# Sigmoid stage of an FFN with fake-quantized activations: six of the twelve gate pieces rounded and multiplied on GpSimd as int32 in place

## The reference

```python
def act_qdq(x):                      # ACT_BITS = 16
    qmax = 2.0 ** (ACT_BITS - 1) - 1.0
    scale = jnp.maximum(jnp.max(jnp.abs(x)) / qmax, 1e-12)
    return jnp.clip(jnp.round(x / scale), -qmax - 1.0, qmax) * scale

def fixed_qdq_u16(x):
    scale = 1.0 / 65536.0
    return jnp.clip(jnp.round(x / scale), 0.0, 65535.0) * scale
...
x = act_qdq(x)
up = act_qdq(x @ lpbq_dequant(w_up).T)
gate = act_qdq(x @ lpbq_dequant(w_gate).T)
sig = fixed_qdq_u16(jax.nn.sigmoid(gate))
gate = act_qdq(gate * sig)
o = act_qdq(gate * up)
return o @ lpbq_dequant(w_down).T
```

## Time and profile before

| | |
|---|---|
| median of 3 runs | 400.63 us |
| profiled execution, span from the first to the last instruction | 398.5 us |
| PE busy | 346.2 us (87%) |
| DVE busy | 330.8 us (83%) |
| ACT busy | 263.0 us (66%) |
| POOL busy | 223.4 us (56%) |
| sigmoid stage, from the gate's scale to `MX2` | 312.0 to 351.9 us |
| `Q` and the reductions | 354.7 to 369.7 us |
| output parts | 372.0 to the end |

### The profile page before, as it was taken

One profiled execution on the slowest core, in us unless ns is written; L12 is line 12 of the kernel. 1 busy time (PEld: TensorE's weight loads), 2 busy tenths in 40 slices (PEclk: granted clock), 3 DMA queues, 4 the chain that ended last, 5 costly groups with the idle time before them and its releaser, 6 DMA issues.

```text
span 398.5 us, 6226 instructions
## 1 busy us (share of the span) xinstructions
PE 346.2 (87%) x1754; PEld 285.0 (72%) x1754; DVE 330.8 (83%) x700; ACT 263.0 (66%) x339; POOL 223.4 (56%) x400
## 2 busy tenths in 40 slices
PE   8979967999999999999999989999999971005997
PEld 7657744768898989989898977777677650003897
DVE  4588558975999999999999989765689899979894
ACT  3655687866576565666656544555467899999650
POOL 2656885897466473847465023222195568992462
PEclk9998999999999999999999999999999996555999
DMA  6998993955353443535332005100000000000022
GB/s 173 341 398 301 326 314 118 315 161 212 112 202 111 151 168 117 201 106 187 132 127 84 3 2 160 51 2 0 1 2 0 1 0 1 0 0 2 0 108 105
DMA packets 19850, 47.77 MB, mean 120 GB/s; under 512 B 2787, under 2 KB 8934, under 8 KB 17254
## 3 DMA queue, kind: packets, MB, share of 16 engines
q1 hardware_dynamic: 18342, 47.16, 33.8%
q10 hardware_dynamic: 1472, 0.20, 0.3%
HBM read 33.10 MB, written 12.58 MB: 115 GB/s over the span
## 4 chain that ended last, share of the span: by engine, by line
PE 59%; DVE 15%; POOL 8%; issue 6%; DMA 6%; ACT 5%; ACTq 0%; DVEq 0%; SPq 0%; POOLq 0%
PE ps L378 57%; DVE S L755 3%; DMA wscr<-wst 2%; POOL XCh L1542 2%; POOL wst L1545 2%; DMA wdr<-n_L_cond_skill_down_dram 2%; DVE O_i L752 1%; PE ps L375 1%; DMA bsr<-in_L_cond_Bs_dram 1%; DVE G L746 1%; ACT U L1307 1%; POOL C_i L1542 1%; ACT ps L1307 1%; DVE Hl L746 1%; DVE HbS L746 1%
## 5 line engine op out<-in xcount | busy, mean ns | idle before, releaser
L1626 POOL CAST xg<-XT 128x64 fp32r x264 | 81.3, 356 | 52.6 <-DVE Hl L746 25.5
L378 PE MATMUL ps<-xg,Wr 128*128 128x384 f32 (+1 forms) x480 | 98.6, 354 | 0.3 <-issue 0.3
L378 PEld LDWEIGHTS ps<-xg,Wr 128*128 128x128 f32 x480 | 85.8, 188 | 7.5 <-issue 0.6
L1307 ACT ACTIVATE Hh<-HbS 128x512 fp32r<-128x512 f32 (+2 forms) x72 | 56.5, 785 | 46.2 <-DVE HbS L746 45.9
L746 DVE TENSOR_TENSOR HbS<-Gb,ps 128x512 f32<-128x512 f32 (+2 forms) x72 | 63.2, 878 | 21.7 <-PE ps L378 18.6
L1307 ACT ACTIVATE Gb<-ps 128x512 f32<-128x512 f32 (+2 forms) x72 | 54.1, 751 | 30.5 <-PE ps L378 28.7
L746 DVE TENSOR_TENSOR Hl<-HbS,Hh 128x768 fp32r<-128x768 f32 (+2 forms) x57 | 55.2, 969 | 2.3 <-ACT Hh L1307 1.8
L752 DVE SCALAR_TENSOR_TENSOR C<-ps,Wt,C 128x32 f32 x264 | 52.4, 279 | 2.9 <-PE ps L378 2.6
L378 PE MATMUL ps<-XT,SHh 128*128 128x512 f32 x128 | 45.7, 398 | 0.8 <-DVE XT L746 0.4
L1545 POOL TENSOR_TENSOR Hl<-HbS,Hh 128x512 fp32r<-128x512 f32 x15 | 19.7, 1316 | 47.0 <-ACT Hh L1307 46.9
L1307 ACT ACTIVATE ps<-G,S 128x1024 int32<-128x1024 f32 (+1 forms) x29 | 35.6, 1250 | 6.7 <-DVE O_i L752 5.7
(11 more groups left out here) (222 smaller groups left out, 675.7 us busy)
## 6 DMA issues: line engine op xcount, KB each, us to landing
Wr<-wscr SPq DMA_DIRECT2D x20, 1024.0 KB, 4.8
wscr<-wst SPq DMA_DIRECT2D x16, 512.0 KB, 5.9
stg<-n_L_cond_skill_gate_dram SPq DMA_DIRECT2D x8, 256.0 KB, 7.6
stg<-in_L_cond_skill_up_dram SPq DMA_DIRECT2D x8, 256.0 KB, 7.9
wdr<-n_L_cond_skill_down_dram SPq DMA_DIRECT2D x8, 256.0 KB, 5.8
xscr<-X SPq DMA_DIRECT2D x8, 256.0 KB, 6.1
X<-xscr SPq DMA_DIRECT2D x8, 256.0 KB, 4.3
out_dram<-X SPq DMA_DIRECT2D x7, 256.0 KB, 2.0
```

What stands on the lines that cost most here:

```text
L378: return e.matmul(o_, l, r, start=start, stop=stop, skip_group_check=True)
L1307: return e.activation(o_, i_, func, **kw)
L1626: last = e.tensor_copy(xg[:, i % XR, :, T * s:T * s + T].rearrange("p a t -> p a t"), XT[:, :, :, bass.ds(regs[s - a_], 1)].rearrange("p a ...
```

## The change

`POOLED` goes from three pieces (3, 6, 9) to six (2, 4, 5, 7, 9, 10). A pooled piece is now an int32 throughout, in the bytes where its float32 stood: POOL rounds `G` to int32 in place, rounds the sigmoid to int32 in place in `tS` (with a limit of 65535 where a zero was added), and multiplies int32 by int32 in place. The conversions back to float32 are gone, six instructions in all, and so are the copies in `C_i`. ACT rounds six pieces where it rounded nine, and DVE multiplies six where it multiplied nine. Everything that reads a pooled piece afterwards (`m`, `Q`, and the first ACT step of the output) reads it as int32. Piece 11 is no longer split into halves. Since a column part j of G holds pieces of both types, ACT makes it in two or three instructions where it made it in one. The four order strings are written anew, except `PE_ORDER`.

```diff
-        POOLED = (3, 6, 9)
+        POOLED = (2, 4, 5, 7, 9, 10)
+        Gi = Gf.bitcast(I32)
+        tI = tS[:, :, :].bitcast(I32)
...
-        DVE_ORDER = ("gtop gsc r0 r1 r2 r3 y0 m0 r5 r4 y1 r6 m1 y2 r8 r7 r9 y4 r10 r11 um y5 utop m2 usc m4 y7 m3 m5 y8 m7 "
+        DVE_ORDER = ("gtop gsc r0 r1 r2 y0 m0 r3 y1 r4 m1 y3 r5 m3 r6 r7 r8 r9 r10 r11 um m4 utop m5 usc y6 y8 m7 m2 m6 m8 "
...
-        OF = {0: 2, 1: 3, 2: 2, 4: 3, 5: 2, 7: 1, 8: 3, 10: 2, 11: 0}
+        OF = {0: 2, 1: 3, 3: 2, 6: 2, 8: 3, 11: 1}
+        def runs(j):
+            kinds = [4 * q + j // 2 in POOLED for q in range(3)]
+            cuts = [q for q in range(3) if q == 0 or kinds[q] != kinds[q - 1]] + [3]
+            return [(a_, b_, kinds[a_]) for a_, b_ in zip(cuts, cuts[1:])]
...
-                    before = {0: (a_g, 11), 1: (a_g, 13), 7: (a_u, 12), 11: (d_sc, USC)}
-                    after = {2: 0, 4: 1, 5: 2, 8: 4, 10: 5}
+                    before = {0: (a_g, 11), 1: (a_g, 13), 11: (a_u, 12)}
+                    after = {3: 0, 6: 3, 8: 1}
...
-                    do(tS[:, p % 4, c], (C_i[:, pc(POOLED.index(p))] if p in POOLED else sloti(OF[p]))[:, c],
-                       ACT.Sigmoid, scale=col(SG_)).then_inc(a_sig, 1)
+                    do(tS[:, p % 4, :], Gi[:, pc(p)] if p in POOLED else sloti(OF[p]), ACT.Sigmoid, scale=col(SG_)).then_inc(a_sig, 1)
...
-                do(part(j, 0, 4), G[:, :, cols(j)], ACT.Identity, scale=col(I2)).then_inc(a_sgn, 1)
+                for a_, b_, whole in runs(j):
+                    g = G[:, a_:b_, cols(j)]
+                    last = do(part(j, 0, 4)[:, a_:b_, :], g.bitcast(I32) if whole else g, ACT.Identity, scale=col(I2))
+                last.then_inc(a_sgn, 1)
...
                 if kind == "q":
-                    w.wait_ge(d_xcl, (2, 4, 5)[k])
-                    ts(C_i[:, pc(k)], Gf[:, pc(p)], col(IG), 0.0).then_inc(k_gq, 1)
-                    w.wait_ge(k_gq, pooled_nth(step))
-                    ts(Gf[:, pc(p)], C_i[:, pc(k)], 1.0, 0.0).then_inc(k_gf, 1)
+                    ts(Gi[:, pc(p)], Gf[:, pc(p)], col(IG), 0.0).then_inc(k_gq, 1)
                 elif kind == "t":
-                    ts(t_i[:, p % 4, c], tS[:, p % 4, c], 65536.0, 0.0).then_inc(k_t, 1)
                     if p in POOLED:
-                        w.wait_ge(k_t, nth(POOL_ORDER, step))
-                        ts(tS[:, p % 4, :], t_i[:, p % 4, :], 1.0, 0.0).then_inc(k_tf, 1)
+                        ts(tI[:, p % 4, :], tS[:, p % 4, :], 65536.0, 65535.0, MUL, ALU.min).then_inc(k_t, 1)
+                    else:
+                        ...
+                        ts(t_i[:, p % 4, :], tS[:, p % 4, :], 65536.0, 0.0).then_inc(k_t, 1)
                 elif kind == "y":
-                    e.tensor_tensor(Gf[:, pc(p)], Gf[:, pc(p)], tS[:, p % 4, :], MUL).then_inc(k_y, 1)
+                    e.tensor_tensor(Gi[:, pc(p)], Gi[:, pc(p)], tI[:, p % 4, :], MUL).then_inc(k_y, 1)
```

More of the change, by code:

```diff
@@ L232, in program @@
             sem(n) for n in ("p_g", "a_g", "p_u", "a_u", "d_mxg", "d_mxu"))
-        a_gq, k_gq, k_gf, a_sig, k_t, k_tf, d_y, k_y, d_my, a_ua, k_uq, a_yq, d_o = (
-            sem(n) for n in ("a_gq", "k_gq", "k_gf", "a_sig", "k_t", "k_tf", "d_y", "k_y", "d_my", "a_ua", "k_uq", "a_yq", "d_o"))
+        a_gq, k_gq, a_sig, k_t, d_y, k_y, d_my, a_ua, k_uq, a_yq, d_o = (
+            sem(n) for n in ("a_gq", "k_gq", "a_sig", "k_t", "d_y", "k_y", "d_my", "a_ua", "k_uq", "a_yq", "d_o"))
         a_sgn, d_oi, k_of, p_out, d_out = (
@@ L333, in program @@
         PIECE = [4 * q + jp for q, jp in ORDER]
-        POOLED = (3, 6, 9)
+        POOLED = (2, 4, 5, 7, 9, 10)
         Uf = U[:, :, :].rearrange("p k n -> p (k n)")
         Gf = G[:, :, :].rearrange("p k n -> p (k n)")
+        Gi = Gf.bitcast(I32)
+        tI = tS[:, :, :].bitcast(I32)
         U_if = U_i[:, :, :].rearrange("p q n -> p (q n)")
         PE_ORDER = "u0 u1 gt gsp u2 u3 u4 u5 u6 u7 u8 u9 u10 u11 ut usp".split()
-        ACT_ORDER = ("e0 e1 q0 e2 s0 e3 e4 q1 e5 s1 q2 e6 s2 e7 s3 e8 q4 e9 s4 e10 q5 e11 s5 q7 s6 q8 s7 q10 s8 A4 s9 A7 "
-                     "s10 q11 A2 s11a A10 s11b A5 A1 A9 A8 A3 A6 A0 Q0 Q1 Q2 Q3 Q4 Q5 Q6 Q7 Q8 Q9 Q10 A11 Q11").split()
-        DVE_ORDER = ("gtop gsc r0 r1 r2 r3 y0 m0 r5 r4 y1 r6 m1 y2 r8 r7 r9 y4 r10 r11 um y5 utop m2 usc m4 y7 m3 m5 y8 m7 "
-                     "m6 m8 y10 m10 y11b y11a m9 m11a m11b").split()
-        POOL_ORDER = "q6 t0 q3 t1 t2 q9 t3 t4 y3 t5 t6 t7 y6 t8 t9 t10 y9 t11a t11b v0 v1 v2 v3 v4 v5 v6 v7 v8 v9 v10 v11".split()
-        OF = {0: 2, 1: 3, 2: 2, 4: 3, 5: 2, 7: 1, 8: 3, 10: 2, 11: 0}
+        ACT_ORDER = ("e0 e1 q0 e2 s0 s2 q1 e3 s1 s4 q3 e4 s3 e5 e6 s5 e7 e8 q6 e9 e10 s7 e11 q8 s6 s8 q11 s9 s10 A9 s11 A4 A1 "
+                     "A2 A6 A10 A0 A5 A3 A8 A7 Q0 Q1 Q2 Q3 Q4 Q5 Q6 Q7 Q8 Q9 Q10 A11 Q11").split()
+        DVE_ORDER = ("gtop gsc r0 r1 r2 y0 m0 r3 y1 r4 m1 y3 r5 m3 r6 r7 r8 r9 r10 r11 um m4 utop m5 usc y6 y8 m7 m2 m6 m8 "
+                     "y11 m11 m9 m10").split()
+        POOL_ORDER = ("q7 q2 t0 t2 q4 q9 t1 q5 q10 t4 t3 t5 y2 y5 y4 t7 t6 t8 y7 t9 t11 y9 t10 y10 "
+                      "v0 v1 v2 v3 v4 v5 v6 v7 v8 v9 v10 v11").split()
+        OF = {0: 2, 1: 3, 3: 2, 6: 2, 8: 3, 11: 1}
         def nth(order, step):
@@ L1219, in _ @@
             for step_ in DVE_ORDER:
-                kind, h = step_[0], step_[-1] if step_[-1] in "ab" else ""
+                kind = step_[0]
                 if step_ == "gtop":
@@ L1250, in _ @@
                     else:
[L1251 to L1254, removed]
+                        w.wait_ge(d_y, nth(DVE_ORDER, f"y{p}"))
+                    red(S[:, G2M + p:G2M + p + 1], (Gi if p in POOLED else Gf)[:, pc(p)], ALU.max, True).then_inc(d_my, 1)
+            w.wait_ge(d_my, 12)
+            red(col(MX2), S[:, G2M:G2M + 12], ALU.max).then_inc(d_col, 1)
             top(4, bank[7])
@@ L1499, in _ @@
             for step in ACT_ORDER:
-                kind, h = step[0], step[-1] if step[-1] in "ab" else ""
-                p = int(step[1:].rstrip("ab"))
+                kind, p = step[0], int(step[1:])
                 if kind == "e":
@@ L1512, in _ @@
                 elif kind == "s":
-                    c = HALF[h]
                     if p in POOLED:
@@ L1666, in _ @@
                 elif kind == "t":
-                    w.wait_ge(a_sig, nth(ACT_ORDER, "s" + step[1:]))
-                    if p >= 4:
-                        w.wait_ge(*((k_y, pooled_nth(f"y{p - 4}")) if p - 4 in POOLED else (d_y, nth(DVE_ORDER, f"y{p - 4}"))))
-                    ts(t_i[:, p % 4, c], tS[:, p % 4, c], 65536.0, 0.0).then_inc(k_t, 1)
+                    w.wait_ge(a_sig, nth(ACT_ORDER, step.replace("t", "s")))
                     if p in POOLED:
-                        w.wait_ge(k_t, nth(POOL_ORDER, step))
-                        ts(tS[:, p % 4, :], t_i[:, p % 4, :], 1.0, 0.0).then_inc(k_tf, 1)
+                        ts(tI[:, p % 4, :], tS[:, p % 4, :], 65536.0, 65535.0, MUL, ALU.min).then_inc(k_t, 1)
+                    else:
+                        for o_ in (p - 4, p - 8):
+                            if o_ >= 0 and o_ not in POOLED:
+                                w.wait_ge(d_y, nth(DVE_ORDER, f"y{o_}"))
+                        ts(t_i[:, p % 4, :], tS[:, p % 4, :], 65536.0, 0.0).then_inc(k_t, 1)
```

26 lines of the change are left out of this document (11 added, 15 removed).

## The result

The changed kernel took 411.37 us (median of 4 runs, 410.69 to 412.50) against 400.79 before in the same comparison: a ratio of 1.0273, 95% interval 1.0241 to 1.0304. I had forecast 398.7 us, with a range up to 400.9. It is 10.6 us slower where I expected 1.9 us less.

What follows compares the result with a forecast made beforehand. It took ACT and DVE, both full in the sigmoid stage, as the bound. An earlier `MX2` reduce (-1.94 us) and the tail (+0.05) gave -1.9, so 398.7 us from 400.6; the 8-in-10 range was 397.8 to 400.9.

Steps and rivals of the forecast that it cites:

- the price of the limited rounding: Pooled `t` on POOL, rounding with a limit: two operations, so 1.045 us as for the existing `t`.
- the upper bound: POOL's new forms: slowest elementwise row, 1.98 us for 480 elements, 4.2 us for 1024; set aside because it compares.
- the same working: Sigmoid stage: new POOL, ACT and DVE orders laid end to end at row prices, 0.04 us per release between engines.
- One sign that I had named for being wrong: End of the sigmoid stage: the forecast is wrong if `m10` on DVE waits over 0.5 us for `y10`.
- a form dearer than its break-even: Rival on POOL: a new instruction form costs more than its break-even price, making the kernel slower; chance 0.12.
- The rival named the multiply first: POOL's int32 multiply is dearer than 2.35 us, break-even at 2.87; dearer roundings or `t` likewise; chance 0.12 together.
- as laid out: Sigmoid stage: DVE gaps early, ACT free 1.2 us before `Q`, POOL 0.7 us in hand, `MX2` reduce 1.94 us earlier.
- DVE's sum: DVE's stage: 30 whole instructions (33.9), 1.0 for small steps and 2.6 of waits, from 312.20 to `m10`'s end at 349.88.
- before's 2.81 us for that stretch: From DVE's `MX2` reduce to the first `Q` on ACT: a fixed string of small steps, 2.81 us.
- one block: From the first `Q` to the end: everything moves forward together by what the sigmoid stage gains.
- PE's clock: Rival: PE idles before `u5` and `u6`, its clock falls to 1.2 GHz; 399.8 to 401.1 us; chance 0.15.
- Tail: Output: ACT makes parts of G in two or three instructions, +0.05 us, with 0 and 0.3 as ends.

Runs made afterwards that it cites:

- e4: Changed kernel with eleven forms of POOL `tensor_scalar`, twice each, added behind POOL's last instruction to price each form; 472.61 us, one execution.
- e1: Changed kernel with the limit at 65535 taken away, the pooled `t` adding zero again; 399.75 us, ratio to before 0.9972.
- e2: Changed kernel with the limit made in two steps, rounding to uint16 and then converting to int32; 402.14 us, ratio to before 1.0048.
- e3: Kernel before with only the limit added to its three pooled sigmoids, written as uint16 and not in place; 407.21 us, ratio 1.0155.
- e5: e1 with four one-column DVE products reading their second factor as a scalar operand; 398.27 us, ratio to before 0.9936.

## Why the prediction was wrong, step by step

**The step that failed** is the price of the limited rounding: "Rounding with a limit instead of an added zero: again two operations, so 1.045 as for `t`." It is 3.63 us. I had the row that told of it and used it as the upper bound only, with the argument "that row compares, and none of the new ones does". In e4 a minimum, a comparison and even a subtraction cost the same, 3.63 to 3.64 us. All cheap `tensor_scalar` rows of POOL in the stage were multiply with add, and I should have taken them as the price of that pair alone. By elements, `tmpP` gave 4.2 us and the truth was 3.63. With the right price the same working gives 10.9 us more than before; measured are 11.5 to the first `Q`, 11.1 to the first `O_i`, and 10.6 in the time. e1, e2, e3 and e4 show it four ways. One sign that I had named for being wrong came with it: `m10` waits for `y10`, 4.86 us where I had set 0.5.

**The chances.** I gave 0.12 to a form dearer than its break-even. The rival named the multiply first, and it was exactly 2.35. All three unrecorded forms I had priced by nearby types and sizes, and too little by the operation.

**DVE, ACT and POOL as laid out.** Right: without the limit, `y0` waits 0.65 us (0.72), `y1` 0.65 (0.73), `r4` 0.36 (0.49), `y3` 0.30 (0.33), and ACT has 1.15 us free ahead of `Q` (1.2). The int32 maxima on DVE cost what the float32 ones did (340.49, 1.22 us in the changed kernel). The printed terms of DVE's sum give 349.7 and not 349.88; those 0.15 us change nothing here.

**Missed: two small instructions on DVE.** No term of the sum was for the products of one column. With the new orders one of them falls under a POOL multiply and ends 1.3 us later. In e1 the `MX2` reduce comes 1.1 us later than laid out, and by the rows this is the reason. At the first `Q` only 0.6 us of that are left, because the two products behind `MX2` took 0.28 us in place of the 0.81 of before, which was luck: I had kept before's 2.81 us for that stretch. e5 shows that the scalar operand takes the 1.3 us off the product; what it is worth in the time, its runs don't tell apart from the clock.

**Missed: the way from the first `Q` to the output.** I let it move forward as one block. It took 17.3 us in before, 17.0 in the changed kernel, 17.9 in e1 and 17.0 in e5, with PE's 17 matmuls and the clock under them. In e1 this is 0.5 us of the missing gain, and in the changed kernel it gave 0.4 us back.

**PE's clock.** The rival was right in its place and its cause: in the profiles of the changed kernel, e1, e2 and e5 the clock fell at the two gaps that I had named, against the forecast of 1.00 up to 331. Except in e2 it fell at the first gap already, under `u5`, and I had priced `u6` to `u8`. Its price depended on how long the clock stayed down: 0.25 us of waiting on ACT in e1, where only `u5` was slow, and 1.10 us in e5, where `u5`, `u6` and the start of `u7` were. It doesn't explain the 10.6 us: POOL, on which they arise, waits only 0.9 us for sigmoids in the changed kernel's stage. (The profile gives 1.30 us for the idle time that I put at 1.5 before.)

**Tail.** I took +0.05 with an upper end of 0.3. From the first `O_i` to the end of the span the changed kernel takes 26.6 us (409.0 less 382.4) and before 26.5 (398.5 less 372.0). ACT's three pieces of an output part run 1.91 us as expected (1.95), and PE's last 144 matmuls have no break.

## What to carry to other kernels

A form of instruction that the trace doesn't show is one unknown for each operation in it, not for its bytes: price the operation from the nearest row *of its kind*, and where six copies of it stand in line on an engine with 0.7 us in hand, measure it first. When an order is written for engines that are all full, a small slip anywhere becomes time; read the tiny instructions on the full engines too. And a free engine's idle time counts against new work only where it lies behind the point at which the work comes in.

## What the runs showed that I had not expected

POOL's `tensor_scalar` has one cheap pair of operations among those tried, multiply and add (1.05 us for 1024 elements). With subtract, min, max or is_equal in the pair it takes 3.63 to 3.64 us, and with min alone 2.77. The int32 multiply costs what the float32 one does (2.353 and 2.351 us).

A column product on DVE with two inputs in SBUF doesn't finish while POOL is in a multiply or a cheap rounding. In e1 it took 1.53 us and ended 0.02 us after POOL's multiply, and in e2 it took 0.56 us and ended with POOL's `t`, at 341.11. With its second factor as a scalar operand it took 0.21 us under a POOL multiply (e5). The Trainium skill (SBUF — State Buffer, "Who interferes with whom") says this of DVE instructions with two SBUF inputs against GpSimd instructions that read SBUF. These traces agree, with one exception, for which the measurement decides: beside a slow `tensor_scalar` the same product took its usual time. This is the timeline of the changed kernel, where POOL is in a limited `t` from 340.54 to 344.17:

```profile
340.54 3.63 POOL L1549 TENSOR_SCALAR tS<-tS 128x1024 int32<-128x1024 f32 x1
...
343.38 0.16 DVE L755 TENSOR_TENSOR S<-S 128x1 f32<-128x1 f32 x1
```

In e3 it is the same (0.16 us at 340.85, with POOL's `t` from 337.75 to 341.38). Two places are few; why it is so stays open.
